# A four-layer graph network on one core: edges counted and ranked on TensorE, given rows filled in between the first scatters, blank rows given different indices

## The chip, the cores and the metric

The kernel runs on one core of one Trainium2 chip. The metric is the device time of one execution in microseconds (us); it is read beside one profiled execution, whose trace gives start, duration and releaser of every instruction.

## The reference

There are 3,125 nodes with 160 features (64 scalars and 32 vectors of 3) and 100,000 edges with a source and a destination; the destinations are sorted, the sources random. Four graph layers follow each other, each on the normalized and rectified node features, and each adds to the node features. What matters here is the common pattern:

```python
h = jnp.maximum(_layernorm(x, axis=-1), 0.0)
w = act(edge_features @ W_fc1) @ W_fc2           # layers 0, 1, 3
y = (h @ W)[gather_index]                        # a row of the node table per edge
m = products(w, y, edge_vector)                  # message of each edge
agg = segment_sum(m, scatter_index, num_segments=N)
x = x + combine(agg @ W_out, h @ W_skip)
```

Layer 0 sums over the source and gathers by the destination; layers 1 to 3 gather by the source and sum over the destination.

## The kernel before, in words

Nodes are split into bins of 32 (`BINS` is 100). Edges must lie in *tiles* of 128 that touch one bin only, so that a one-hot matrix of 128 x 32 on TensorE can sum them. There are 880 tiles in 110 groups of 8. A tile that is not full ends in *blank rows*, with key -1; tiles that no bin needs are blank in whole and stand last. Edges are held as 128 partitions by 782 columns, cut into 34 *chunks* of 23 columns (`CHUNK`, `CHUNKS`).

**Prologue.** VectorE finds for every edge its slot (`pos_i`). `places(o)` counts the edges of every bin per partition (L1011, one compare with an accumulated sum for each of 100 bins), TensorE sums the counts over partitions (L1402, L1403), and VectorE works out the first slot of every bin and the tables of tiles. `rank` then goes over the bins in fours: a mark of 0 or 1 (L1058), a running sum of the marks that starts at the bin's base (L1062, into PSUM), the last column carried to the next segment (L1069), and a copy of the sums where the mark is set (L1070). The 782 columns are ranked in three *segments*, which end at chunks 6, 18 and 34 (`SEGMENTS`); `positions` turns ranks into slots. Order o = 0 is by source, o = 1 by destination.

With the slots, ScalarE's `fill` puts edge vector, index and key into a staged chunk (L794 to L800), and GpSimd's `scatter` writes it, one indirect DMA of 128 rows per column (L670, 782 in all), into `rows_a`, which a large DMA on ScalarE's queue has cleared to blank rows (L751, semaphore `s_init`). SP stages the chunks (`stage_rows`, L530). The rows of layers 1 to 3 are already sorted: `given` on SP (L481 load, L485 store) and `complete` on ScalarE (L761, L763) put index and key into each chunk of them and store it to `rows_given`, two buffers in turn; `copy_tiles` later copies runs of 128 of these into tiles (L463). Tiles without edges copy a blank row block. `starts` and `bins_out` on SP send the tables of tiles through DRAM (L506, L520, L521, L523). ScalarE goes on to the chunks from the seventh (`COPY_FROM`) only after segment 1, all given rows and the tile starts (`s_starts`). If the destinations are not sorted (`flag`), the second order is ranked too, and placed by GpSimd. From chunk 18 on, node statistics and the first node table are worked out beside the fills.

**Layers.** In each, an edge phase of 110 groups: SP loads a group of rows, GpSimd gathers 8 times 128 rows of the node table by their index (L739), ScalarE turns marks into selections (L866), TensorE makes weights and sums (L1484, L1507, L1509, in layer 2 L1503), VectorE the products (L1209, L1213) and the sum over tiles (L1197). Two buffers of 8 tiles hold the gathered rows. A node phase follows (L1549, L1557). Queues work in program order; all waits are semaphores written by hand.

The few lines that set the order around the change, on DVE:

```python
places(0)
segment(0)
# falls, then
places(1)
segment(1)
segment(2)
statistics()
prep_first()
```

Of the kernel before, what the change touches and what calls it, by code (L numbers as in the profile page):

```python
# [55 lines left out]
WAYS = 4  # L56
assert BINS % WAYS == 0
WORK = 2 * PRODS * 320 + 2 * 1024
assert WORK >= 2 * PRODS * 416 + 2 * 512
PREP_FROM = SEGMENTS[2]  # L60

# [146 lines left out]
def gnn_program(nc, t):  # L208

    ctx = ExitStack()  # L210
    with ctx:
# [71 lines left out]
        def bank(i, p, a, b):  # L283
            return pb[i][0:p, a:b]
# [17 lines left out]
        eq = [carve(even // 2).bitcast(I16)[:, 0:COLS] for _ in range(WAYS)]  # L302
        zero_h = carve(even // 2).bitcast(I16)[:, 0:COLS]
# [4 lines left out]
        pos_f = [sh2[:, k * COLS:k * COLS + COLS] for k in range(3)] + [carve(COLS)]  # L308
        tri, ones = carve(P), carve(P)
        count, ntile, first_tile, bins_f, bins_z, pad = (carve(BINS) for _ in range(6))  # L310
        base = [carve(BINS) for _ in range(2)]
# [5 lines left out]
        bins_i = carve(BINS).bitcast(I32)  # L317
        tile_id, tile_bin = carve(TCOLS), carve(TCOLS)
        tile_bin_i = carve(TCOLS).bitcast(I32)
# [5 lines left out]
        s_in = sem("s_in")  # L325
# [15 lines left out]
        s_cnt = [sem(f"s_cnt{o}") for o in range(2)]  # L341
        s_cum = [sem(f"s_cum{o}") for o in range(2)]
        s_eq = [sem(f"s_eq{o}") for o in range(2)]
        s_scan = [sem(f"s_scan{o}") for o in range(2)]
        s_pick = [sem(f"s_pick{o}") for o in range(2)]
# [6 lines left out]
        s_again = sem("s_again")  # L352
# [11 lines left out]
        s_ranked = sem("s_ranked")  # L364
# [105 lines left out]
        def _(sp):  # L470
            sp.dma_start(key_i[0], t["skey"]).then_inc(s_in, 16)
            sp.dma_start(sh, t["edge_attr_3"]).then_inc(s_in, 16)
            sp.dma_start(key_i[1], t["dkey"][0:P * COLS].rearrange("(p c) -> p c", p=P)).then_inc(s_in, 16)
            sp.dma_start(key_next, t["dkey"][1:P * COLS + 1].rearrange("(p c) -> p c", p=P)).then_inc(s_in, 16)
# [27 lines left out]
            def bins_out(o):  # L502

                sp.wait_ge(s_tb[o], 1)
                with nc.allow_non_contiguous_dma(reason="one word per tile"):
                    sp.dma_start(bins_dram[o].rearrange("(c p) -> p c", p=P), tile_bin_i).then_inc(s_tbd[o], 16)  # L506
# [18 lines left out]

# [1113 lines left out]
```

## Time and profile before

| | |
|---|---|
| median of 3 runs | 6326.96 us (6325.39 to 6328.03) |
| profiled execution | 6318.5 us |
| its span | 6316.5 us |
| busy TensorE / VectorE | 4116.9 / 3529.7 us |
| busy ScalarE / GpSimd | 3434.8 / 4217.4 us |
| mean DMA traffic | 80 GB/s |
| first scatter / first gather | 251.4 / 1359.6 us |

The busy times are sums over stages with different limits. The span is to be read in stages: the prologue up to the last scatter, then four times an edge phase and a node phase. PE is TensorE, DVE is VectorE, ACT ScalarE, POOL GpSimd, SP the engine that only issues DMAs; a q behind a name is its queue. Durations of GpSimd's instructions are those of issuing the DMA, not of its transfer.

### The profile page before, as it was taken

How to read it: one execution, taken by the hardware profiler on the slowest of the kernel's cores; microseconds unless marked ns; L12 is line 12 of the kernel's file. 1: busy time of each engine (PE TensorE's matmuls, PEld its weight loads, DVE VectorE, ACT ScalarE, POOL GpSimd, SP SyncE). 2: the span in 40 equal slices, each digit the busy share in tenths (PEclk: the TensorE clock that was granted, in tenths of full speed). 3: DMA queues.
4: the chain of work that ended last, by engine and by line, in shares of the span. 5: the costliest groups of instructions: out<-in, count | busy, mean ns of one | idle time of the engine just before them, and what ended most of it. 6: DMA issues, size and time to landing. Idle time of an engine off the chain costs nothing.

```text
span 6316.5 us, 109949 instructions
## 1 busy us (share of the span) xinstructions
PE 4116.9 (65%) x22628; PEld 3645.2 (58%) x22628; DVE 3529.7 (56%) x10802; ACT 3434.8 (54%) x14704; POOL 4217.4 (67%) x4426
## 2 busy tenths in 40 slices
PE   0000011129999998799999986454545588888887
PEld 0000001129988887688888875444444577777776
DVE  8899400038877776466666655233233356666666
ACT  0000000016666664488888876666666467777773
POOL 2355777767777775177777764777777457777772
PEclk9999999999999999899999997555555699999998
DMA  8321223324444446022222252222222422222234
GB/s 314 109 44 45 71 75 80 77 61 94 94 91 93 92 92 70 27 79 78 79 78 78 79 68 56 79 79 78 79 79 79 43 64 79 78 78 79 79 76 38
DMA packets 660093, 506.69 MB, mean 80 GB/s; under 512 B 445302, under 2 KB 563333, under 8 KB 659894
## 3 DMA queue, kind: packets, MB, share of 16 engines
q0 software_dynamic: 195888, 316.94, 21.5%
q1 hardware_dynamic: 381782, 148.41, 9.7%
q10 hardware_dynamic: 82352, 40.52, 2.2%
q8 instruction: 29, 0.48, 0.0%
q14 instruction: 42, 0.34, 0.0%
HBM read 423.69 MB, written 96.48 MB: 82 GB/s over the span
## 4 chain that ended last, share of the span: by engine, by line
POOL 29%; issue 19%; DMA 13%; PE 11%; DVE 4%; DVEq 1%; SPq 1%; ACT 1%; POOLq 1%; ACTq 0%
POOL gath L739 29%; DMA gath<-table,rows 9%; PE bank L1557 2%; DMA rows<-rows_b 2%; PE bank L1507 2%; PE bank L1484 2%; PE bank L1549 1%; DVE work L1213 1%; DMA rows<-rows_a 1%; PE bank L1509 1%; PE bank L1503 1%; DVE acc L1197 1%; DVE work L1209 1%; DVEq L1220 0%; PE bank L1457 0%
## 5 line engine op out<-in xcount | busy, mean ns | idle before, releaser
L739 POOL DMA_INDIRECT gath<-table,rows x3520 | 3356.7, 954 | 1223.3 <-issue 1004.0
L866 ACT ACTIVATE sel<-acc,rows 128x32 f32<-128x32 f32 x10560 | 2294.1, 307 | 713.0 <-DVE acc L1188 712.2
L1197 DVE TENSOR_TENSOR acc<-acc,bank 128x160 f32 (+1 forms) x3520 | 1208.3, 343 | 1068.7 <-PE bank L1503 704.4
L1507 PE MATMUL bank<-work,sel 128*128 128x160 f32 (+1 forms) x5280 | 1341.5, 336 | 95.9 <-DVE acc L1197 94.7
L1484 PE MATMUL bank<-w,work 128*128 128x224 f32 (+2 forms) x5280 | 1169.0, 344 | 114.3 <-DVE work L1213 104.2
L1509 PE MATMUL bank<-work,sel 128*128 128x160 f32 x5280 | 1156.6, 301 | 0.0
L670 POOL DMA_INDIRECT rows_a<-acc x782 | 770.2, 985 | 528.7 <-ACT acc L800 291.0
L1484 PEld LDWEIGHTS bank<-w,work 128*128 128x128 f32 (+1 forms) x5280 | 894.5, 192 | 261.5 <-DVE work L1213 192.5
L1507 PEld LDWEIGHTS bank<-work,sel 128*128 128x128 f32 x5280 | 886.7, 191 | 193.4 <-DVE acc L1197 167.7
L1209 DVE TENSOR_TENSOR work<-bank,gath 128x256 f32<-128x256 f32 x1320 | 555.7, 421 | 775.2 <-DMA gath<-table,rows 715.6
L1509 PEld LDWEIGHTS bank<-work,sel 128*128 128x128 f32 x5280 | 915.9, 192 | 46.3
L1503 PE MATMUL bank<-gath,sel 128*128 128x160 f32 x1760 | 549.0, 493 | 575.1 <-DMA gath<-table,rows 559.7
L1213 DVE TENSOR_TENSOR work<-bank,gath 128x192 f32<-128x192 f32 (+1 forms) x2640 | 895.3, 381 | 0.0
L1503 PEld LDWEIGHTS bank<-gath,sel 128*128 128x128 f32 x1760 | 462.1, 330 | 661.9 <-issue 645.0
L866 ACT ACTIVATE sel<-sel,rows 128x32 f32<-128x32 f32 x2640 | 581.7, 308 | 53.3 <-DVE sel L1188 45.3
L1377 PE MATMUL bank<-ident,sel 128*64 128x128 f32 x25 | 10.2, 407 | 791.4 <-ACT sel L777 791.4
L1377 PEld LDWEIGHTS bank<-ident,sel 128*64 128x64 f32 x25 | 4.3, 173 | 794.2 <-issue 794.1
L849 ACT ACTIVATE work<-bank 100x512 f32<-100x512 f32 (+1 forms) x440 | 250.9, 596 | 352.3 <-PE bank L1457 229.9
L794 ACT ACTIVATE acc<-acc 128x69 f32 (+1 forms) x34 | 9.3, 273 | 773.6 <-DMA acc<-in_rows_a 583.9
L844 ACT ACTIVATE attrT<-bank 128x256 f32<-128x256 f32 (+1 forms) x330 | 145.4, 441 | 270.4 <-PE bank L1447 226.8
L1460 PE MATMUL bank<-attrT,w 128*100 128x256 f32 x880 | 210.9, 383 | 1.8 <-ACT attrT L844 1.8
L1011 DVE TENSOR_SCALAR_CACHE_REDUCE acc<-acc,iota_bins 128x782 int16<-128x782 bf16 x200 | 193.6, 1024 | 26.5 <-DVE acc L1011 25.8
(216 smaller groups left out, 2961.0 us busy)
## 6 DMA issues: line engine op xcount, KB each, us to landing
gath<-table,rows POOLq DMA_INDIRECT x3520
rows<-rows_b SPq DMA_DIRECT2D x330, 128.0 KB
rows_a<-acc ACTq DMA_DIRECT2D x1, 30360.0 KB, 111.5
rows<-rows_a SPq DMA_DIRECT2D x110, 256.0 KB
acc<-in_rows_a SPq DMA_DIRECT2D x34, 793.5 KB, 4.5
acc<-in_rows_b SPq DMA_DIRECT2D x34, 368.0 KB, 3.5
rows_given<-acc SPq DMA_DIRECT2D x34, 368.0 KB, 3.9
rows_a<-acc POOLq DMA_INDIRECT x782
```

The lines of the kernel that those rows point to most:

```text
L670: pool.indirect_dma_start(rows_dram[0][:, :], bass.IndirectOffsetOnAxis(ap=pos_r[q][:, u:u + 1], axis=0), stage[0][q][:, u * A_W:(u + 1) * ...
L739: pool.indirect_dma_start(gath[q][:, u, :], None, table_dram[n][:, :], bass.IndirectOffsetOnAxis(ap=flat[:, u * w + first:u * w + first + ...
L849: i = act.activation(hid_t(n, q)[0:hrows, 512 * b:512 * b + 512], bank(2 + b, hrows, 0, 512), ACT.Silu if n == 3 else ACT.Relu, scale={0: ...
L866: i = act.activation(sel[q][:, t, at:at + BIN], hot, ACT.Copy, scale=e[:, k:k + 1])
L1197: dve.tensor_tensor(sums, sums, bank(6 + b, P, 256 * h, 256 * h + L.width), ALU.add).then_inc(S["fl"].sem, 1)
L1209: dve.tensor_tensor(ps, wt[:, :, 0:128].rearrange("p h (w c) -> p h w c", w=2), two[:, :, 0:S0].unsqueeze(2).to_broadcast([P, 2, 2, S0]), ...
L1213: ins = dve.tensor_tensor(pv, wt[:, h, 128:L.wcols].rearrange("p (w m) -> p w m", w=nv) .unsqueeze(2).to_broadcast([P, nv, 3, V1]), two[:, ...
L1460: i = pe.matmul(bank(2 + k // 2, 100, 256 * (k % 2), 256 * (k % 2) + 256), w1[1][:, k, :], attrT[:, 0:256], start=True, stop=True)
L1484: ins = pe.matmul(bank(4 + u % 2, P, 224 * h, 224 * h + L.wcols), hid, w, start=True, stop=True, skip_group_check=True)
L1503: ins = pe.matmul(out, sel[qv][:, t, 0:128], gath[qv][:, t, :], start=True, stop=True, skip_group_check=True)
L1507: pe.matmul(out, sel[qv][:, t, 96:224], work[:, a + NF:a + NF + L.width], start=True, stop=False, skip_group_check=True)
L1509: ins = pe.matmul(bank(6 + b, P, 256 * h, 256 * h + NF), sel[qv][:, t, 0:128], work[:, a:a + NF], start=False, stop=True, skip_group_check ...
```

## The change

**Counting.** A mark (`mark`, L1034 of the kernel after) is one compare into one of 8 bfloat16 buffers in `work`. For each bin TensorE multiplies the 782 marked columns by a matrix whose only column of ones is the bin's (`one_at`, L1438, L1439), so that two PSUM banks collect a count per bin and column over all partitions. VectorE runs the sum along the columns (`bases`, L1066, L1068), gets the tiles per bin, has TensorE sum those, and subtracts the columns' own counts, which gives a base per bin and column.

**Ranking.** For each bin TensorE multiplies the marks by a triangle of ones in bfloat16 (`tri_h`, L1459), which counts the marked edges in the partitions above, and adds the bin's row of bases in float32 (L1460); VectorE copies the result where the mark is set (L1122), now into one array `pos_f`. Four PSUM banks and a lead of four marks stand between them. The scans, the carries, the four partial arrays and their clearing go. The segments end at chunks 4, 18 and 34.

**Order.** VectorE waits for the source keys alone before it counts; the work on the edge vectors lies between the marks of the first count. The second order is always ranked, before the node statistics. SP loads the first chunks and the nodes first, and starts the given rows after `s_init`; ScalarE completes 10 given chunks after its second fill and 6 after each of the third to sixth.

**Blank rows** get an index of their own, 3(8p + t) for partition p and tile t of a group, in place of 0.

```diff
-SEGMENTS = (0, 6, 18, CHUNKS)
-COPY_FROM = SEGMENTS[1]
+SEGMENTS = (0, 4, 18, CHUNKS)
+COPY_FROM = 6
+GIVEN_FIRST, GIVEN_EACH = 10, 6
+MARKS, PREFIXES, AHEAD = 8, 4, 4
+PAD_STEP = NODES // (P * GT)
...
+            for o, k in enumerate((A_IDX, B_IDX)):
+
+                pool.iota(blank[o].rearrange("p (t c) -> p t c", t=GT)[:, :, k].bitcast(I32), pattern=[[PAD_STEP, GT]], base=0,
+                          channel_multiplier=PAD_STEP * GT).then_inc(s_blank, 1)
...
-            sp.wait_ge(s_in, 64)
-            pipeline(sp, CHUNKS, 2, 0, 1, given)
+            for c in range(2):
+                stage_rows(c, 0, c)
...
+            sp.wait_ge(s_init, 16)
+            step = 0
+            for c in range(2, COPY_FROM):
+                for _ in range(GIVEN_FIRST + 1 if c == 2 else GIVEN_EACH):
+                    given(step, step // 2, step % 2)
+                    step += 1
+                stage_rows(c, c // 2, c % 2)
+            for step in range(step, CHUNKS + 1):
+                given(step, step // 2, step % 2)
...
+            def mark(o, b, lo, hi):
+
+                e = marked[0]
+                wait(dve, s_used, e - MARKS + 1)
+                dve.tensor_scalar(marks[e % MARKS][:, 0:hi - lo], bin_h[o][:, lo:hi], iota_bins[:, b:b + 1], None,
+                                  ALU.is_equal).then_inc(s_mark, 1)
+                marked[0] += 1
...
+            def rank(o, lo, hi):
+
+                first = marked[0]
+                for b in range(BINS + AHEAD):
+                    if b < BINS:
+                        mark(o, b, lo, hi)
+                    if b >= AHEAD:
+                        r = picked[0]
+                        mask = marks[(first + b - AHEAD) % MARKS].bitcast(I16)[:, 0:hi - lo]
+                        wait(dve, s_prefix, r + 1)
+
+                        wait(dve, s_pick, r)
+                        dve.copy_predicated(pos_f[:, lo:hi], mask, bank(4 + r % PREFIXES, P, 0, hi - lo)).then_inc(s_pick, 1)
+                        picked[0] += 1
+                wait(dve, s_pick, picked[0])
...
+            count(0)
+            bases(0)
...
             segment(0)
-
+            tiles(0)
+            segment(1)
...
+            count(1)
+            bases(1)
+            tiles(1)
             segment(2)
+            for half in range(2):
+                rank(1, half * (COLS // 2), (half + 1) * (COLS // 2))
+            positions(1, 0, COLS)
+            dve.wait_ge(s_pos[1], 1)
...
+            def rank(o, lo, hi):
+
+                for b in range(BINS):
+                    wait(pe, s_mark, used[0] + 1)
+                    wait(pe, s_pick, ranked[0] - PREFIXES + 1)
+                    out = bank(4 + ranked[0] % PREFIXES, P, 0, hi - lo)
+                    pe.matmul(out, tri_h, marks[used[0] % MARKS][:, 0:hi - lo], start=True, stop=False).then_inc(s_used, 1)
+                    pe.matmul(out, ident[0:BINS, b:b + 1].to_broadcast([BINS, P]), base[o][0:BINS, lo:hi],
+                              start=False, stop=True).then_inc(s_prefix, 1)
```

SP's queue at the start of the program, before (the given rows are loaded into and stored from `acc`; between these rows the loop over the other given chunks is left out):

```order
L474 DMA acc<-in_dkey 128x782
L481 DMA acc<-in_rows_b 128x736 x2
L485 DMA rows_given<-acc 128x736
...
L489 DMA x<-in_x 128x25x160
L492 DMA attr<-in_node_vec 128x25x1
L506 DMA tile_bins<-acc 128x7x1
L530 DMA acc<-in_rows_a 128x1587 x2
```

The same place in the kernel after, up to the third chunk's load and then from the last given stores to the tables:

```order
L486 DMA acc<-in_dkey 128x782
L492 DMA acc<-in_rows_a 128x1587 x2
L507 DMA x<-in_x 128x25x160
L510 DMA attr<-in_node_vec 128x25x1
L499 DMA acc<-in_rows_b 128x736 x2
L503 DMA rows_given<-acc 128x736
...
L492 DMA acc<-in_rows_a 128x1587
...
L503 DMA rows_given<-acc 128x736 x2
L534 DMA tile_bins<-acc 128x7x1 x2
L548 DMA tile_starts<-acc 128x7x1
```

The rows of the first two chunks and the nodes moved ahead of the given rows, and the tables of tiles to behind all of them.

VectorE in the ranking of the first segment, before, the end of one round over four bins (the scans write `bank`, a PSUM bank each):

```order
L1058 TENSOR_SCALAR acc<-acc,iota_bins 128x138
L1062 ISA
L1062 SCALAR_TENSOR_TENSOR bank<-acc 128x138
...
L1069 COPY acc<-bank 128x1
L1070 COPY_PREDICATED acc<-acc,bank 128x138
```

And after, from the bases (L1066 to L1080) into the ranking (`work` holds the marks):

```order
L1066 SCALAR_TENSOR_TENSOR work<-bank,acc 100x512
L1068 SCALAR_TENSOR_TENSOR work<-bank,work,acc 100x270
...
L1076 TENSOR_SCALAR acc<-bank 100x1
L1080 SCALAR_TENSOR_TENSOR acc<-work,acc,bank 100x92
...
L1034 TENSOR_SCALAR work<-acc,iota_bins 128x92 x5
L1122 COPY_PREDICATED acc<-work,bank 128x92
```

Of four instructions per bin two are left, and what they read from `bank` now comes from TensorE's L1459 and L1460.

## Rows read from the trace of the kernel before

**Rows 1.** Page, costliest groups: GpSimd's gathers; busy us, mean ns, idle before.
```profile
L739 POOL DMA_INDIRECT gath<-table,rows x3520 | 3356.7, 954 | 1223.3 <-issue 1004.0
```

**Rows 2.** Timeline of GpSimd, 250:555: start us, us, line, [idle before <-releaser].
```profile
251.40 1.29 POOL L670 DMA_INDIRECT rows_a<-acc  x1 [196.97 <-ACT acc L800]
...
522.48 1.15 POOL L670 DMA_INDIRECT rows_a<-acc  x1 [94.03 <-ACT acc L800]
```

**Rows 3.** Windows, the scatters alone: stretch, us, busy, clock, DMA share, GB/s.
```profile
554.00:709.00 155.00, 120.14 (x115) 1.00 0.28 70
710.00:1350.00 640.00, 486.69 (x504) 1.00 0.30 75
```

**Rows 4.** Timeline of VectorE, 11:250.
```profile
11.13 2.60 DVE L963 TENSOR_TENSOR acc<-acc 128x2346 f32<-128x2346 f32 x1 [11.00 <-DMA acc<-in_dkey]
...
25.19 0.71 DVE L1090 MEMSET acc<- 128x782 f32 x1 [0.23 <-DVE acc L967]
...
142.74 0.26 DVE L1016 TENSOR_SCALAR acc<-bank 128x100 int32<-128x100 f32 x1 [1.33 <-PE bank L1403]
...
249.17 0.30 DVE L1086 TENSOR_TENSOR acc<-acc 128x138 int32<-128x138 int32 x1
```

**Rows 5.** Groups by shape, VectorE, 0:700: marks L1058 and picks L1070.
```profile
L1070 DVE COPY_PREDICATED acc<-acc,bank 128x368 f32<-128x368 int16 x100 | 47.4, 550 | 0.0
...
L1070 DVE COPY_PREDICATED acc<-acc,bank 128x138 f32<-128x138 int16 x100 | 28.1, 302 | 0.0
...
L1058 DVE TENSOR_SCALAR acc<-acc,iota_bins 128x368 int16<-128x368 bf16 x100 | 25.6, 319 | 10.5 <-DVE acc L1070 10.2 <-DVE acc L1086 0.2
...
L1058 DVE TENSOR_SCALAR acc<-acc,iota_bins 128x138 int16<-128x138 bf16 x100 | 19.1, 256 | 12.8 <-DVE acc L1070 12.5 <-issue 0.2
```

**Rows 6.** Timeline of TensorE, 2060:2066, edge phase 0 at full clock.
```profile
2061.18 0.59 PE L1507 MATMUL bank<-work,sel 128*128 128x256 f32 x2
2061.61 0.43 PE L1509 MATMUL bank<-work,sel 128*128 128x160 f32 x2
```

**Rows 7.** Page, DMA issues: KB each, median us from issue to landing.
```profile
rows_a<-acc ACTq DMA_DIRECT2D x1, 30360.0 KB, 111.5
...
acc<-in_skey SPq DMA_DIRECT2D x1, 391.0 KB, 3.1
```

**Rows 8.** Timeline of SP's queue, 20:410: given-row loads, tile tables, next rows.
```profile
27.23 0.36 SPq L481 DMA_DIRECT2D acc<-in_rows_b  x1
...
109.87 0.34 SPq L481 DMA_DIRECT2D acc<-in_rows_b  x1
...
213.39 0.34 SPq L481 DMA_DIRECT2D acc<-in_rows_b  x1
...
370.67 0.38 SPq L506 DMA_DIRECT2D tile_bins<-acc  x1
383.37 0.38 SPq L520 DMA_DIRECT2D tile_starts<-acc  x1
...
400.46 0.38 SPq L530 DMA_DIRECT2D acc<-in_rows_a  x1
```

**Rows 9.** Windows, GpSimd, in edge phase 1: middle and end.
```profile
3600.00:3650.00 50.00, 37.82 (x41) 1.00 0.28 78
3720.00:3785.00 65.00, 38.32 (x41) 0.89 0.90 56
```

**Rows 10.** Timeline of GpSimd, 6143:6218, the last 47 gathers of phase 3.
```profile
6143.81 0.95 POOL L739 DMA_INDIRECT gath<-table,rows  x1 [0.30 <-issue]
...
6217.22 0.95 POOL L739 DMA_INDIRECT gath<-table,rows  x1 [0.30 <-issue]
```

**Rows 11.** Chain that ended last, 6120:6225: start us, us, what.
```profile
6132.54 2.54 DMA gath<-table,rows
...
6212.18 9.65 DMA gath<-table,rows
```

**Rows 12.** Windows, all engines, edge phase 2; clock behind the busy times.
```profile
3900.00:4900.00 1000.00, 497.91 (x1599) 419.20 (x1598) 300.21 (x995) 686.28 (x3191) 757.20 (x797) 0.50 0.28 78
```

More of the change, by code:

```diff
@@ L572, in _ @@
             bins_out(0)
-            for c in range(2):
-                stage_rows(c, 0, c)
-            pairs(sp, 2, COPY_FROM, stage_rows)
             bins_out(1)
@@ L1028, in places, with tiles @@
+            def tiles(o):
+                dve.wait_ge(s_rows, o + 1)
+                link(dve.tensor_copy(ntile, bank(3, P, 0, BINS)))
+                link(dve.tensor_copy(first_tile, bank(3, P, 128, 128 + BINS)))
                 for c in range(TCOLS):
@@ L1392, in prep_first @@
                 pipeline(pe, BLOCKS, 3, 2, 1, body)
-            for o in range(2):
-                if o:
-                    pe.wait_ge(s_falls, 1)
-                    pe.matmul(bank(1, 1, 0, 1), falls, ones[:, 0:1], start=True, stop=True).then_inc(s_flag_sum, 1)
-                    pe.wait_ge(s_tb[0], 1)
-                pe.wait_ge(s_cnt[o], BINS)
-                pe.matmul(bank(0, P, 0, BINS), tri, count, start=True, stop=True)
-                pe.matmul(bank(0, P, 128, 128 + BINS), ones, count, start=True, stop=True).then_inc(s_cum[o], 1)
+            used, ranked = [0], [0]
@@ new lines, in count @@
+            def count(o):
+                for b in range(BINS):
+                    wait(pe, s_mark, used[0] + 1)
+                    seen = marks[used[0] % MARKS]
+                    row = one_at[:, BINS - 1 - b:2 * BINS - 1 - b]
+                    pe.matmul(bank(0, BINS, 0, BANK), row, seen[:, 0:BANK], start=b == 0, stop=b == BINS - 1)
+                    ins = pe.matmul(bank(1, BINS, 0, COLS - BANK), row, seen[:, BANK:COLS], start=b == 0, stop=b == BINS - 1)
+                    ins.then_inc(s_used, 1)
+                    used[0] += 1
+                pe.wait_ge(s_total, o + 1)
+                pe.matmul(bank(2, BINS, 0, 1), tri[0:BINS, 0:BINS], tiles_of[0:BINS, :], start=True, stop=True).then_inc(s_first, 1)
@@ new lines, in rank @@
+            def rank(o, lo, hi):
+                for b in range(BINS):
+                    wait(pe, s_mark, used[0] + 1)
+                    wait(pe, s_pick, ranked[0] - PREFIXES + 1)
[3 more added lines that the diff above has]
+                              start=False, stop=True).then_inc(s_prefix, 1)
+                    used[0] += 1
+                    ranked[0] += 1
@@ new lines, in _ @@
+            count(0)
+            pe.wait_ge(s_base[0], 1)
+            rank(0, 0, SEGMENTS[1] * CHUNK)
+            rows_of(0)
+            pe.wait_ge(s_base[0], 3)
+            rank(0, SEGMENTS[1] * CHUNK, SEGMENTS[2] * CHUNK)
+            pe.wait_ge(s_falls, 1)
+            pe.matmul(bank(3, 1, 0, 1), falls, ones[:, 0:1], start=True, stop=True).then_inc(s_flag_sum, 1)
+            count(1)
+            rows_of(1)
+            rank(0, SEGMENTS[2] * CHUNK, COLS)
+            pe.wait_ge(s_base[1], 3)
@@ L1405, in _ @@
+            for half in range(2):
+                rank(1, half * (COLS // 2), (half + 1) * (COLS // 2))
             pe.wait_ge(s_flag, 1)
```

235 lines of the change are left out of this document (113 added, 122 removed).

## Prediction

> **What bounds the kernel now.** I first asked which engine has no slack. In the costliest groups GpSimd's gathers stand alone: 3,520 of them at 954 ns, and most of the idle time before them is called issue, 1004.0 us [rows 1], 0.30 before each [rows 10]. So one gather costs 1.255 us, 47 of them 59, and the four edge phases (880 each) run at GpSimd's pace. Ahead of them stand the 782 scatters. GpSimd's timeline shows the first at 251.40 after 196.97 us of idling, and another stop of 94.03 before 522.48, between the 138th and the 139th; ScalarE ended both [rows 2]. Undisturbed, a scatter takes 640/504 = 1.27 us, a chunk of 23 of them 29.2; while VectorE ranks the last segment it is 155/115 = 1.35 [rows 3]. 251.4 + 94 + 34 x 29.2 + 11 for the disturbed chunks is 1349 (by the same sum 1149 after), and edge phase 0 follows. So the prologue is worth two stops, and what sets them is VectorE, which counts and ranks until 249.17 [rows 4] and again before the second stop. The last place is the end of each edge phase, below.
>
> **Counting and ranking, up to the first scatter.** Sizes 138 and 368 give prices [rows 5]. A mark (compare, bfloat16 in, 16 bits out) takes 191 to 256 ns of VectorE, 0.28 ns a column: 178 ns for 92 columns, 243 for 322, 262 for 391, 373 for 782. 
>
> VectorE no longer waits for all four loads (11.00 us [rows 4]): the source keys land 3.1 us after an issue at 0.9 [rows 7], and two casts make it 6. Marks: 100 x 0.373 = 37. The edge-vector work, 11.13 to 25.19 [rows 4], is only moved in between: 14. Bases: eight short instructions at the 0.26 us of L1016, one round trip through TensorE at its 1.33 us [rows 4], and 1,564 columns of scan and subtraction, which I put at 2 ns each: 6.5. Ranking four chunks, not six: 100 x (0.178 + 0.252) = 43. Positions, six instructions of 0.25: 1.5. From their end to the first scatter it was 249.47 to 251.40, 1.9. Sum: 6 + 37 + 14 + 6.5 + 43 + 1.5 + 1.9 = 110. The clearing of the scattered rows took until 2.4 + 111.5 = 114 [rows 7], beside ten given-row steps that now wait for it; so it ends earlier, and is the second limit. I take 111. **Gain: 251.4 - 111 = 140.** Bounds: 98 (no gap between instructions, half the bases) and 131 (slow TensorE).
>
> **The second stop.** Segment 1 (14 chunks) needs 100 x 0.74 = 74 and is ranked by about 190; the chunks before it last until 111 + 4 x 29.2 = 228. That stop goes. What is late next is SP's queue. The given-row steps, once ahead of the ranking, now lie after the first two fills, behind the wait for the clearing, and SP cannot send the tile tables before the last of them. A step took (213.39 - 109.87)/22 = 4.7 us without the clearing beside it, and (109.87 - 27.23)/9 = 9.2 with it [rows 8]. From the second fill at 112: 34 x 4.7 = 160, so 272; chunks 2 to 5 come in time, since each needs six steps, 28 us, of a 29.2 us chunk. Then the first tile table, 12.7, and from the second table's issue to the next load of rows 400.46 - 370.67 = 29.8 [rows 8]; in both kernels ScalarE's seventh fill needs all that. With the load (under one step, 4.7) and the fill, 1.9: 321. GpSimd is through six chunks at 111 + 175 = 286. **Stop 35 for 94: gain 59.** Bounds: 0 and 80. VectorE's part of the tables (second count, bases, tiles: 55 us after segment 1) is done by 245, 40 before SP asks for it; were SP faster, the stop would end with VectorE, near 0.
>
> The second ranking, once skipped for sorted keys, now always runs: 2 x 100 x 0.84 = 168 us. VectorE is then free at about 495; the node preparation needs it at chunk 18, 321 + 12 x 29.2 = 671. Hidden by 176 us. Nothing on GpSimd's own queue changes but two short iotas and the blank index columns. The disturbed scatters: 115 x 0.08 = 9 us before; after the stop 170 us of ranking remain at the same 6%: 10. **Zero.** The Trainium skill, SBUF — State Buffer, section "Who interferes with whom", says that a VectorE compare in a 2-port mode shuts GpSimd out for the whole instruction, and descriptor writing with it. By it the stretch would be dearer than the rows say; that is a rival.
>
> **Blank rows.** They all held source index 0, now 128 different ones. About 40 wholly blank tiles end each edge phase. There the DMA engines are busy 0.90 of the time for 56 GB/s, against 0.28 for 78 in the middle of the phase, and GpSimd issues 41 gathers in 65 us, not in 50 [rows 9]: the transfers are slow, not many. In the last phase the 47 gathers from 6143.81 to 6217.22 take 73.4 us instead of 59, 14.4 too many [rows 10]; the same two rows of the other three give 19.5, 14.5 and 14.9. Sum 63. A late gather then lands 9.65 us after its start, an ordinary one 2.54 [rows 11]; some 5 of these 7 us are left at each end, 20. I take all of it, as the index is the one thing that sets these rows apart. **Gain: 83.** Bounds: 0 and 92.
>
> **Sum.** 6318.5 - 140 - 59 - 0 - 83 = 6036.5 by the profiled execution's own time. The median of the runs stands 8.5 above it, so 6045. No change could be told from one of 0.2%, about 13 us.
>
> **Rivals.**
> - *TensorE stays at the low clock in the prologue.* In edge phase 2 it is busy 498 of 1000 us and granted 0.50, 1.2 GHz [rows 12]; in ranking 92 columns it would be busy under half of the time. Against it: counting keeps it busy 0.33 of 0.37 us, and while it idles in the scatters the page still prints 1.00 [rows 3], which settles nothing. At half the clock counting takes 65 us, 322 columns 134: first scatter at 131, segment 1 at 275 against 248, tile tables only at 352, seventh chunk at 387 instead of 321: +66, 6111. Chance 0.10. The Trainium skill, TensorE: Matmul & The Clock Gate, Part 1, says that the low clock is the default and work releases it; the trace agrees as far as phase 2 goes.
> - *Given-row steps slowed by the scatters beside them*, at 6 to 9.2 us instead of 4.7: 34 times 1.3 to 4.5, +45 to +150, 6090 to 6195. For it the 9.2 beside the clearing; against it, the scatters load the engines far less. Chance 0.10.
> - *GpSimd shut out by every mark.* 200 marks of 0.26 us in the stretch after the stop are 52 instead of 10: +42, 6087. The scatters at 1.35 us [rows 3], beside as many marks as that per column, speak against it. Chance 0.06.
> - *Blank rows were not the cause*, the slow tails stay: 6045 + 83 = 6128. Chance 0.06.
> - *The stop vanishes too* (the small tables land faster once nothing is queued ahead): 6010. Chance 0.05.
> - *Slower than before: the hand-over doesn't pipeline.* VectorE and TensorE now exchange two signals per bin in 700 bins; four banks and a lead of four marks hide this. If every pick waited for a round trip, 1.33 us [rows 4] beside its own work, VectorE would be free only at 25 + 700 t, and the 15 chunks from the node preparation on come after it, 440 us. That passes the old end of 1353 plus the 83 of the tails from t = 1.4 us a bin; at 1.7 it ends at 1655, +505 against my 1150: 6550. The lead in the code speaks against it. Chance 0.03.
>
> **Chances.** The forecast itself has 0.60, within 6005 to 6080 by its own bounds. The range that leaves out 2 in 10 takes in the vanished stop, the shut-out and part of the slow steps and the low clock: 5995 to 6112. Faster 0.96, same 0.01, slower 0.03.
>
> **What would show it.** First scatter near 111 (98 to 131); 0.37 us per mark of 782 columns and TensorE not ending VectorE's waits in counting; one stop near 35 us before the 139th scatter, ended by ScalarE with the tile tables behind it; the last scatter near 1150; the 47 last gathers of each phase in 59 to 62 us, at a DMA share near 0.3. A first scatter past 131, steps over 5 us on SP, or tails still at 73 us would make it wrong.

## The result, and the profile after

The changed kernel takes **6037.2 us** (median of 4 runs, 6032.0 to 6039.1) against 6326.2 us before (6323.1 to 6328.0): ratio **0.954, interval 0.9525 to 0.9553**. The forecast was 6045, range 5995 to 6112. The profiled execution has a span of 6037.4 us, 279.1 less than before.

Two of the four terms came out as forecast, one was 16 us too large, and one of zero was a net gain of 9. Timeline of GpSimd after the change (start us, us, line, operation, idle before and its releaser), at the first scatter, at the stop between the 138th and the 139th, at the last scatter and at the last gather:

```profile
127.53 1.10 POOL L697 DMA_INDIRECT rows_a<-acc  x1 [67.81 <-ACT acc L824]
...
342.38 0.97 POOL L697 DMA_INDIRECT rows_a<-acc  x1 [35.27 <-ACT acc L824]
...
1160.76 0.97 POOL L697 DMA_INDIRECT rows_a<-acc  x1 [0.30 <-issue]
1168.28 1.00 POOL L766 DMA_INDIRECT gath<-table,rows  x1 [6.55 <-DMA rows<-rows_a]
...
5945.32 0.95 POOL L766 DMA_INDIRECT gath<-table,rows  x1 [0.30 <-issue]
```

The first scatter moved from 251.40 to 127.53 (-123.9), the wait of 94.03 became 35.27 [rows 2], the last scatter moved from 1352.4 to 1160.76 (-191.6), the last gather from 6217.22 [rows 10] to 5945.32. The wait is ended by the same partner as before, ScalarE's fill. Of the 191.6 the first scatter gives 123.9 and the stop 58.8. The other 9 are a difference: the scatters behind the stop, which the ranking no longer disturbs, take 11.5 us less, and the first 138 take 2.5 us more than before (experiment 3 says why). From the last scatter to the last gather it took 4864.8 us and now takes 4784.6 (-80.2), and from there to the end 99.3 and now 92.1 (-7.2).

Windows of GpSimd (stretch, its length, busy with count, granted clock, DMA share, GB/s), first two with scatters, where rows 3 stood at 115 and 504 of them, then the middle and the end of edge phase 1, where rows 9 stood at 0.28 and 0.90:

```profile
554.00:709.00 155.00, 117.81 (x123) 0.50 0.30 73
710.00:1130.00 420.00, 319.35 (x331) 0.50 0.32 78
...
3000.00:3050.00 50.00, 37.84 (x40) 1.00 0.31 77
3490.62:3548.62 58.00, 43.98 (x46) 1.00 0.29 77
```

The last 47 gathers of the four phases take 59.1, 59.2, 59.1 and 59.3 us, before 79.1, 73.5, 73.9 and 73.4; the DMA engines are now no busier there than in the middle.

SP's queue before the stop (start us, us, line, what moves):

```profile
294.59 0.33 SPq L499 DMA_DIRECT2D acc<-in_rows_b  x1
295.03 4.19 SPq L503 DMA_DIRECT2D rows_given<-acc  x2
299.27 12.92 SPq L534 DMA_DIRECT2D tile_bins<-acc  x2
321.05 0.36 SPq L548 DMA_DIRECT2D tile_starts<-acc  x1
321.46 2.85 SPq L549 DMA_DIRECT2D tile_first_node<-acc  x1
334.75 0.29 SPq L551 DMA_DIRECT2D acc<-tile_starts  x1
336.51 0.41 SPq L492 DMA_DIRECT2D acc<-in_rows_a  x1
```

The last given rows are stored at 295 to 299 (forecast 272, from a start at 112); then three landings of small tables follow each other, and only then come the rows of the seventh chunk. The forecast's order is there, 20 us later, as its start is 16 later.

**Why the first scatter is at 127.5 and not at 111.** Timeline of VectorE, ahead of the count, between count and ranking, and at the end of the first segment:

```profile
4.31 5.31 DVE L1056 TENSOR_SCALAR acc<-acc 128x782 int32<-128x782 int32 x1 [4.18 <-POOL acc L662]
...
10.26 3.10 DVE L1034 TENSOR_SCALAR work<-acc,iota_bins 128x782 bf16<-128x782 bf16 x9
...
60.57 1.22 DVE L1066 TENSOR_TENSOR_SCAN work<-bank,acc 100x512 f32<-100x512 f32 x1 [0.63 <-PE bank L1439]
...
65.33 0.86 DVE L1034 TENSOR_SCALAR work<-acc,iota_bins 128x92 bf16<-128x92 bf16 x5
...
123.92 0.26 DVE L1122 COPY_PREDICATED acc<-work,bank 128x92 f32<-128x92 int16 x1 [0.32 <-PE bank L1460]
```

The count starts at 10.26 and not at 6: a shift of 782 integers takes 5.31 us beside GpSimd's fillings (4.22 to 9.79 us), where the like of it at 49.19 takes 0.56. Count and edge vectors take 50 us against 51, the bases 4.8 against 6.5. Then a hundred bins of 92 columns take 58.9 us against 43, and the picks wait for TensorE. Windows of all engines (TensorE's matmuls and weight loads, VectorE, ScalarE, GpSimd, then clock): the whole count, a part of it, the gap behind it, the first ranking, and the second segment's:

```profile
10.00:60.00 50.00, 39.91 (x198) 21.65 (x199) 49.06 (x107) 0.85 (x1) 44.04 (x74) 0.93 1.07 388
36.00:42.00 6.00, 5.63 (x17) 3.57 (x18) 5.55 (x16) 0.00 (x0) 6.00 (x10) 0.50 1.08 391
64.00:65.00 1.00, 0.00 (x0) 0.00 (x0) 0.96 (x4) 0.00 (x0) 0.00 (x0) 0.50 1.07 389
66.00:73.00 7.00, 7.00 (x37) 6.98 (x38) 4.81 (x25) 0.00 (x0) 0.00 (x0) 0.50 1.06 383
73.00:106.00 33.00, 33.00 (x172) 32.89 (x172) 23.27 (x115) 0.00 (x0) 0.00 (x0) 0.50 0.93 331
136.00:138.00 2.00, 2.00 (x11) 1.22 (x10) 2.00 (x7) 0.04 (x1) 1.39 (x3) 1.00 0.87 314
```

In the ranking TensorE is busy without a gap and granted 0.50, the 1.2 GHz level: 0.59 us a bin. The clock had fallen before the ranking's first product at 65.72, in the gap. The count has a smaller case of the same: VectorE's reciprocal (30.82 to 35.86 us) leaves TensorE with 1.5 us of work between 30 and 36, and 36 to 42 is granted 0.50. Groups by shape in 66:123 (busy us, mean ns, idle before and releasers):

```profile
L1460 PE MATMUL bank<-acc,ident 100*128 100x92 f32 x198 | 57.5, 458 | 0.0
...
L1122 DVE COPY_PREDICATED acc<-work,bank 128x92 f32<-128x92 int16 x98 | 25.5, 260 | 17.2 <-PE bank L1460 17.1
L1034 DVE TENSOR_SCALAR work<-acc,iota_bins 128x92 bf16<-128x92 bf16 x97 | 23.4, 242 | 0.0
```

VectorE waits 17.2 us for the bases' float32 matmul. Against the forecast's terms that is +4.3 (start), -0.7 (count), -1.7 (bases), +15.9 (bins), -0.1 (positions and fill): 17.6 over their sum of 109.9, 16.5 over the 111 taken.

### The profile page after: what moved, and what is told of

Same layout as the page of the kernel before. It is cut to its first block, busy times and chain, and to the rows that moved or that the text cites. A ratio compares the mean times of both kernels' runs of the same rounds, so it can differ in the third digit from the quotient of the medians.

```text
span 6037.4 us, 112434 instructions
## 1 busy us (share of the span) xinstructions
PE 4551.9 (75%) x24536; PEld 3911.6 (65%) x24536; DVE 3374.1 (56%) x10505; ACT 3437.0 (57%) x14704; POOL 4216.1 (70%) x4431
## 4 chain that ended last, share of the span: by engine, by line
POOL 26%; issue 17%; PE 15%; DMA 13%; DVE 5%; DVEq 2%; ACT 1%; SPq 1%; POOLq 1%; ACTq 0%
POOL gath L766 26%; DMA gath<-table,rows 11%; PE bank L1582 3%; PE bank L1559 3%; DMA rows<-rows_a 2%; PE bank L1632 2%; PE bank L1584 2%; DVE work L1249 2%; PE bank L1578 2%; PE bank L1624 1%; DVE acc L1233 1%; PE bank L1535 1%; DVEq L1256 1%; DVE work L1245 1%; ACT sel L900 0%
## 5 line engine op out<-in xcount | busy, mean ns | idle before, releaser
L1460 PE MATMUL bank<-acc,ident 100*128 100x391 f32 (+3 forms) x1000 | 374.5, 475 | 0.0
L1122 DVE COPY_PREDICATED acc<-work,bank 128x391 f32<-128x391 int16 (+3 forms) x500 | 253.1, 506 | 34.0 <-PE bank L1460 29.6
```

What stands on the lines that cost most here:

```text
L1122: dve.copy_predicated(pos_f[:, lo:hi], mask, bank(4 + r % PREFIXES, P, 0, hi - lo)).then_inc(s_pick, 1)
L1460: pe.matmul(out, ident[0:BINS, b:b + 1].to_broadcast([BINS, P]), base[o][0:BINS, lo:hi], start=False, stop=True).then_inc(s_prefix, 1)
```

## The experiments

Where nothing else is said, the kernel before took 6320 to 6326 us beside the runs.

### 1. TensorE kept at work between count and ranking

The last product of the count ends at 60.5 us and the first of the ranking starts at 65.7; between them TensorE had 0.5 us of work. Fourteen products into a spare bank fill the gap:

```diff
                     ins.then_inc(s_used, 1)
                     used[0] += 1
+                if o == 0:
+                    for _ in range(8):
+                        pe.matmul(bank(3, P, 0, BANK), tri_h, bin_h[0][:, 0:BANK], start=True, stop=True)
                 pe.wait_ge(s_total, o + 1)
                 pe.matmul(bank(2, BINS, 0, 1), tri[0:BINS, 0:BINS], ...).then_inc(s_first, 1)
+                if o == 0:
+                    for _ in range(6):
+                        pe.matmul(bank(3, P, 0, BANK), tri_h, bin_h[0][:, 0:BANK], start=True, stop=True)
```

> The changed kernel with 14 more bf16 products of 512 columns on TensorE, 8 between the last count and the tiles' sum and 6 behind it, into a spare bank, in the 5 us in which TensorE has almost nothing to do before the first ranking. Theory (the granted clock fell to 0.50 at 73.2 us because TensorE had a gap from 60 to 65 us, and the low clock is why a bin of the first ranking takes 0.58 us instead of 0.43): clock at 1.00 to the end of the first segment, first scatter at 111 to 114 us instead of 127.5; then the first chunks are 15 us earlier, but the stop in front of chunk 6, which ends by SP's queue, takes all of it back: 6037 within 5 us. Rival 1 (the clock falls because of the short float32 products, gap or no gap): first scatter at 127 to 131 us. Rival 2 (the end follows the first scatter, not the queue): 6022.

Measured: 6013.9 us (6012.9 to 6015.2), ratio 0.9514 (0.950 to 0.9529), 23 us under the change as made. The two intervals just overlap (the change as made starts at 0.9525), so what carries this experiment is its trace. Windows of this kernel at the start of the ranking and over it (it ends at 102.4), then the groups:

```profile
66.00:73.00 7.00, 7.00 (x64) 6.60 (x62) 7.00 (x40) 0.00 (x0) 0.00 (x0) 1.00 1.06 380
66.00:102.00 36.00, 35.71 (x301) 32.70 (x299) 35.30 (x194) 0.00 (x0) 0.00 (x0) 1.00 1.04 374
```

```profile
L1466 PE MATMUL bank<-acc,ident 100*128 100x92 f32 x200 | 35.9, 293 | 0.0
...
L1122 DVE COPY_PREDICATED acc<-work,bank 128x92 f32<-128x92 int16 x99 | 25.7, 260 | 0.7 <-PE bank L1466 0.3
```

The granted clock stays at 1.00 (2.4 GHz) through the ranking, although its products are the same short ones; the matmul takes 293 ns and not 458, VectorE's wait is gone, and the hundred bins take from 64.87 to 102.4 us, 0.375 each instead of 0.59. First scatter at 106.12: 21 us earlier, more than expected, as mark and pick follow each other faster than their two durations (0.242 + 0.260) add up to. The profiles repeat it: in the three kernels with the fourteen products the first scatter is at 106.1 to 106.3, in all those that rank and count as changed without them, and keep the order of the given rows, at 127.0 to 127.5. So the gap lowered the clock, and the short float32 products alone don't. The first half of the theory holds. (The expectation says 73.2 us for the fall; the windows show it between 62 and 64 us.) The Trainium skill, TensorE: Matmul & The Clock Gate, Part 1, has the half rate as the state that idleness brings back; by that rule and these windows alike, the work goes into the gap, and not into the ranking. The section also lets activity release the throttle, and there the trace is less simple: the ranking kept TensorE busy all through 66 to 123 us at 0.50, and the clock was back only at 136, beside the next segment's products.

Its second half fell: I expected the stop to take the 21 us back. Its length nearly stayed (61.7 us from the sixth chunk's start to the seventh's, 64.6 in the change as made), and the scatters came 21 us earlier at the first and 24 at the last. The given steps don't start with the clearing but with ScalarE's `complete`, which stands behind the second fill and so behind the ranking; an earlier first scatter moves the whole queue, tables and all.

### 2. The stop before the seventh chunk

First, the small tables between the given steps instead of behind them (SP's order alone, landings waited for where the data are read):

```diff
                 stage_rows(c, c // 2, c % 2)
+                if c == 3:
+                    bins_out(0)
+            bins_out(1)
+            starts_out()
             for step in range(step, CHUNKS + 1):
                 given(step, step // 2, step % 2)
+            starts_in()
```

> The changed kernel with the tile tables' writes issued between the given steps (the bins of ranking 0 after chunk 3's rows, the bins of ranking 1 and the starts after chunk 5's rows, at about 270 us), their landings waited for only where the data are read. Theory (the second stop of 35 us is the queue of SP: six given steps of 5 us from 270 to 295 us and behind them three table landings to 335 us, one behind the other): tables land beside the last steps, the starts row at about 302 to 306 us, chunk 6's first scatter at about 308 to 314 us instead of 342, and 6037 - 28 to 35 = 6002 to 6009 us. Rival (the tables are slow because the DMA engines are full, and only get slower between the given steps): the steps stretch, the scatter of chunk 6 stays at 335 to 342 us, 6030 to 6040 us. Second rival (the scatters are not what the end follows): scatter earlier, time at 6037.

Measured: 6027.5 us (6024.9 to 6031.3), ratio 0.9536 (0.9523 to 0.9549), within the interval of the change as made. In the profile the seventh chunk starts at 328.1 instead of 342.4, but the fourth, fifth and sixth chunk take 33.2, 38.3 and 39.7 us. SP's queue there:

```profile
273.50 0.87 SPq L510 DMA_DIRECT2D tile_bins<-acc  x1
274.41 0.89 SPq L516 DMA_DIRECT2D tile_starts<-acc  x1
275.35 0.88 SPq L517 DMA_DIRECT2D tile_first_node<-acc  x1
276.90 2.56 SPq L499 DMA_DIRECT2D acc<-in_rows_b  x1
287.91 0.35 SPq L503 DMA_DIRECT2D rows_given<-acc  x1
299.96 0.33 SPq L499 DMA_DIRECT2D acc<-in_rows_b  x1
```

The load behind the tables is issued at 276.90 and the next at 299.96, where two steps take 10 us: the tables, one word to each address, cost the given steps 13 us. Of the 28 to 34 us that the theory gave the seventh chunk 14 are left, and in the time they are within the noise.

Then the same four writes on ScalarE's queue, together with experiment 1:

```diff
+                    if c == COPY_FROM - 1:
+                        act.wait_ge(s_start, 1)
+                        act.dma_start(starts_dram.rearrange("(c p) -> p c", p=P), tile_start).then_inc(s_startd, 16)
+                        act.dma_start(first_node_dram.rearrange("(c p) -> p c", p=P), tile_node).then_inc(s_startd, 16)
```

> The changed kernel with the 14 products that fill TensorE's gap, and with the four writes of tile tables (bins, starts, first nodes) issued on ACT's queue behind the rows of chunks 4 and 5 instead of on SP's behind the last given steps. Theory (the gap costs 21 us at the first scatter and all scatters after it, and the stop in front of chunk 6 comes from four one-word-per-tile writes that stand in SP's queue, 10 to 13 us each, after the last given step): first scatter at 106 us, the given steps end at 274 us as without the tables' move, the starts row is read at about 277 us, chunk 6's first scatter at 287 to 292 us instead of 318.6, so 6014 - 26 to 31 = 5983 to 5988 us. Rival (the small writes hold the DMA engines, whichever queue they stand in, as they did between the given steps, where three in a row took 23 us out of the given steps): chunk 6 at 305 to 312 us, 6002 to 6010 us.

Measured: 6019.8 us (6013.4 to 6023.4), ratio 0.9511 (0.9498 to 0.9524); experiment 1 alone had 0.9514. The rival's mechanism holds, and it costs more than the rival said (6002 to 6010 us). SP's queue, with the tables now on the other one (one issued at 222.46, the other three from 262.17 on):

```profile
259.23 0.33 SPq L499 DMA_DIRECT2D acc<-in_rows_b  x1
265.04 0.34 SPq L503 DMA_DIRECT2D rows_given<-acc  x1
284.83 0.33 SPq L499 DMA_DIRECT2D acc<-in_rows_b  x1
```

25.6 us between two loads that are otherwise 5 apart: the writes are no dearer for standing in SP's queue, they hold up the given steps from the other queue too. The seventh chunk starts at 315.1, 3.5 us before that of experiment 1, and not at 305 to 312. The Trainium skill, DMA: Bandwidth & Descriptors, Specifications, gives 512 bytes as the least size of a transfer at full rate, since shorter ones are read, modified and written; these have 4. No run here separates that cause from another, but it fits a cost that goes where the writes go.

Last, the seventh chunk ahead of the tables, again with experiment 1. Its scatter reads nothing of them, only the copies of whole tiles do:

```diff
+            stage_rows(COPY_FROM, COPY_FROM // 2, 0)
             bins_out(0)
             bins_out(1)
             starts()
...
             assert done == CHUNKS
+            fill(COPY_FROM, COPY_FROM // 2, 0)
             act.wait_ge(s_empty, 16)
```

> The changed kernel with the 14 products that fill TensorE's gap (alone 6014 us), and with the rows and the fill of chunk 6 put ahead of the tile tables in SP's and ACT's order; only the copies of whole tiles still wait for the tables and the given rows. Theory (chunk 6 waits for the tables by the order of the two queues alone, since its scatter reads nothing of them, and the small writes cost the same 36 us wherever they stand, but now beside chunk 6's scatter): chunk 6 starts at 286 to 289 us instead of 318.6, chunk 7 follows at about 320 to 325 us (its rows stand behind the tables, which end at about 313 us), so 22 to 28 us of the 32 are kept: 6014 - 22 to 28 = 5986 to 5992 us. Rival (the small writes stretch chunk 6's rows and scatters as they stretched the given steps): chunk 7 at 335 us or later, 6000 to 6014 us.

Measured: 6016.7 us (5999.2 to 6019.5) where the kernel before took 6345.8, so a ratio of **0.9479 (0.9467 to 0.9492)**, the lowest of all: clearly under the change as made (0.9525 at least), and by little under experiment 1 (0.950 at least). Beside a kernel before of 6326 us that ratio is 5997 us, against an expected 5986 to 5992. The profiled execution, the lowest of the five, has a span of 5997.5 us. The seventh chunk starts at 285.2, with no stop; the stop is now before the eighth:

```profile
336.07 0.97 POOL L700 DMA_INDIRECT rows_a<-acc  x1 [21.69 <-ACT acc L827]
```

That is 11 us won and not 22 to 28. The small writes are little of the reason: from the first table's issue to the load of the starts they took 37.8 us, 35.5 in the change as made. SP's queue shows the rest:

```profile
313.85 0.29 SPq L551 DMA_DIRECT2D acc<-tile_starts  x1
317.39 12.47 SPq L475 DMA_DIRECT2D rows_b<-rows_given  x16
329.98 0.52 SPq L492 DMA_DIRECT2D acc<-in_rows_a  x1
```

Sixteen tile copies of the seventh chunk take 12.5 us to issue and stand ahead of the eighth chunk's rows. I had left these out of the expectation. Rows before copies would be the next step; that was not tried.

### 3. The old order around the given rows, and no second ranking

```diff
+            pipeline(sp, CHUNKS, 2, 0, 1, given)
...
-            for c in range(2, COPY_FROM):
-                for _ in range(GIVEN_FIRST + 1 if c == 2 else GIVEN_EACH):
-                    given(step, step // 2, step % 2)
...
+            pairs(act, 0, CHUNKS, complete)
             act.wait_ge(s_pos[0], 1)
```

> The changed kernel with the old order around the given rows: all 34 given steps before the first scatter, not waiting for the clearing, the rows of chunks 2 to 5 after them. The ranking stays as changed. Theory (the interleaving is worth what the given steps would take in front of the first scatter, less the second stop that it causes): the steps run from about 15 us at 4.7 us and more each, beside the clearing, to 190 to 215 us, the first scatter is at 195 to 220 us instead of 127, the stop in front of chunk 6 vanishes (35 us), so +33 to +58: 6070 to 6095 us. Rival (given steps are quick without scatters beside them and end by 130 us): the first scatter stays near 130 us and the stop goes, 6002 to 6015 us, faster than the change as made.

Measured: 6104.6 us (6102.7 to 6108.0), ratio 0.966. First scatter at 226.9, no stop at the seventh chunk, last scatter at 1224.3, 63.6 later than in the change as made: +99.4 at the front, -36 up to the 139th scatter. The direction is the theory's; the front is 7 us past its range, and the time 10, since the steps beside the clearing take 8.2 to 9.6 us each. The interleaving is worth 67 us, over a third of what the prologue gained; faster ranking alone would have left the given rows as the new first wait.

```diff
-            for half in range(2):
-                rank(1, half * (COLS // 2), (half + 1) * (COLS // 2))
             positions(1, 0, COLS)
```

> The changed kernel without the second ranking's 200 picks, marks and products (positions by destination, which are read only when the keys are unsorted; this run leaves them out). Theory (168 us of VectorE work lie wholly beside the scatters, which end at 1161 us): VectorE is done at about 345 us instead of 515, scatters keep 29.3-29.4 us each, and the time is 6037 within 6 us. Rival (the marks in bf16 shut GpSimd out of the shared port and stretch its descriptors): chunks during 345 to 515 us become shorter by 1 to 2 us each, 5 chunks, 6027 to 6032 us.

Measured: 6034.6 us (6032.0 to 6035.8), ratio 0.9547 (0.9532 to 0.9561): no change. Scatters beside the ranking and without it, first the change as made, then this kernel:

```profile
345.00:515.00 170.00, 129.44 (x134) 0.99 0.33 78
```

```profile
345.00:515.00 170.00, 129.35 (x134) 0.50 0.32 77
```

134 scatters in 170 us, 1.27 us each, both times. Some 200 marks of 0.33 us cost GpSimd nothing. Before the change the stretch beside VectorE's ranking had 1.35 us a scatter [rows 3]. Its timeline shows where: in every round of four bins one scatter's issue of five takes 1.39 us and not 0.97, and it is always the one that is under way as the four scans end. One round of the kernel before:

```profile
602.91 0.97 POOL L670 DMA_INDIRECT rows_a<-acc  x1 [0.30 <-issue]
603.35 3.61 DVE L1062 TENSOR_TENSOR_SCAN bank<-acc 128x368 f32<-128x368 int16 x4
605.46 1.39 POOL L670 DMA_INDIRECT rows_a<-acc  x1 [0.30 <-issue]
```

The long issue ends at 606.85, the scans at 606.96; the one at 602.91 runs beside marks (602.40 to 603.43) and takes the usual 0.97. All 20 rounds from 554 to 690 us look like this. So what is gone is the scans, and why they hold up an issue no run here shows.

Marks are not free everywhere. In the second count of the kernel after they follow each other without a gap, 782 columns wide, and there the scatters take 1.03 us to issue and 1.34 from one to the next:

```profile
213.05 28.87 DVE L1034 TENSOR_SCALAR work<-acc,iota_bins 128x782 bf16<-128x782 bf16 x86 [0.16 <-PE bank L1439]
216.29 1.03 POOL L697 DMA_INDIRECT rows_a<-acc  x1 [0.30 <-issue]
```

From 243 us on, with the count over and the DMA engines as busy, it is 1.27 again. That makes 1.8 of the 2.5 us that the first 138 scatters lost.

### 4. The blank rows

```diff
-            for o, k in enumerate((A_IDX, B_IDX)):
-                pool.iota(blank[o]..., pattern=[[PAD_STEP, GT]], base=0, channel_multiplier=PAD_STEP * GT).then_inc(s_blank, 1)
```

> The changed kernel with the blank rows naming node row 0 again, as before the change. Theory (the 5 per cent came from two places, and the blank rows are worth 83 to 92 us of it): the last 47 gathers of each edge phase go back from 59.1-59.3 us to 73.4-79.1 us, the transfers behind each phase grow by 5 to 7 us, and the run takes 6037 + 83 to 92 = 6120 to 6130 us; the first scatter stays at 127 us. Rival (the tails became shorter because the phases start and end at other moments, not by the blank rows): within 5 us of 6037.

> The kernel before the change with the spread blank rows alone. Theory (both gains add up, since the tails lie behind each other in the chain and nothing of the ranking reaches them): 6326 - 83 to 92 = 6234 to 6243 us, first scatter still at 251 us. Rival (the gain of the blank rows needs the new ranking): within 5 us of 6326.

> The changed kernel with all blank rows naming one node row in the middle of the table (5000) and not row 0. Theory (what costs is that all blank rows read the same row, whichever): tails of 73 to 79 us and 6120 to 6130 us, as with row 0. Rival (row 0 is special, by its place at the start of the table): 6037 us.

> The changed kernel with eight rows for the blanks: the 128 partitions of one gather all read the same row, the eight gathers of a group read eight rows that lie 1,250 apart. Theory A (it is the repeat inside one gather that costs, 128 descriptors on one row): as slow as with one row for all, tails of 73 to 79 us, 6120 to 6130 us. Theory B (it is the repeat over all transfers in flight, so one row in eight gathers is an eighth of the crowd): most of the gain stays, tails of 59 to 63 us, 6037 to 6055 us.

The middle row is 1562 and the eight rows lie 390 apart, since there are 3,125 nodes; the expectations name wrong numbers. These four were made in one session in which everything that moves data was slower: the kernel before took 8461.8 us (8426 to 8478), groups of gathers 12.9 to 15.1 us on average over a phase, instead of 10. They took 8381.5, 8428.5, 8357.3 and 8347.8 us. The second, the kernel before with spread rows, is faster by 33 us there (ratio 0.9972, 0.9955 to 0.999), not by 83 to 92, for at that pace 47 ordinary gathers take 76 to 89 us themselves, as long as the tails. What can still be read is edge phase 0: its last 47 gathers take 92.8 us with row 0, 90.7 with one row in the middle, 81.0 with eight rows and 79.1 spread (this last in the kernel before; the second and third come from one run each). By that, row 0 is not special. Whether the two gains add up as exactly as the theory says stays open at the ordinary pace; it wasn't tried again.

> The changed kernel with the blank rows naming node row 0 again, a second time: the first time the four runs on blank rows were made where the kernel before took 8462 us and a group of gathers 14.6 to 15 us, so that nothing of 6037 us can be read from them. Theory, as before: the last 47 gathers of each edge phase go back from 59.1-59.3 us to 73.4-79.1 us, and where the kernel before takes 6320 to 6326 us the run takes 6037 + 83 to 92 = 6115 to 6130 us. Rival (the tails are shorter by the phases' other timing): within 5 us of the change as made.

Measured: 6114.5 us (6106.7 to 6127.3), ratio 0.9671 (0.9655 to 0.9688), 77 us over the change as made. Tails of 86.3, 72.3, 77.6 and 74.0 us: +73.5 in sum, and the stretches behind the four phases are 5.7, 6.1, 1.9 and 5.5 us longer: 92.7. Against it stand a stop 7 us shorter and groups of gathers at 10.018 us instead of 10.061, 4 us a phase (last section). The profiled spans differ by 70.0.

> The changed kernel with eight rows for the blanks (one row for all 128 partitions of one gather, the eight gathers of a group on eight rows), a second time, where groups of gathers take 10 us. With row 0 for all the last 47 gathers take 86.3, 72.3, 77.6 and 74.0 us and the run 6114 us. Theory A (the repeat inside one gather costs, and row 0 is nothing special): tails of 72 to 86 us, 6105 to 6125 us. Theory B (the repeat over all transfers in flight costs, or row 0's place does): tails of 59 to 63 us, 6037 to 6055 us.

Measured: 6126.1 us (6122.9 to 6129.1), ratio 0.9653 (0.9638 to 0.9667), with the kernel before at 6345.8. The total fits A, the phases say something else. Tails of 60.5, 74.6, 75.3 and 75.8 us. Windows of GpSimd over the last 47 gathers of phases 0 and 1:

```profile
2239.52:2298.72 59.20, 44.47 (x47) 1.00 0.64 88
3501.60:3574.93 73.33, 43.94 (x47) 0.86 0.82 56
```

and phase 0 with row 0 everywhere:

```profile
2225.82:2310.86 85.04, 43.83 (x47) 0.86 0.79 60
```

Only phase 0 reads the eight rows. In layers 1 to 3 blank tiles are copies of one 128-row block of `rows_given`, made from the first of the eight columns (`blank[1][:, 0:B_W]`), which in this variant is row 0 throughout. So phase 0 is the test, and it says B: 128 descriptors on one row cost 1.4 us over the spread rows in 47 gathers, if the next gather goes to another row; the DMA engines are still twice as busy (0.64 for 88 GB/s). Phases 1 to 3 repeat the case of row 0. In the change as made these phases read 128 rows, the same in all eight gathers (24p by the change's formula, not 3(8p + t)), and are fast.

## Why the prediction was right, point by point

- **First scatter, gain 140: it was 123.9.** The step "Then TensorE needs 0.33 us per bin in counting ..." held in counting (the marks wait 0.7 us for TensorE there), and the choice of the lower price was right for wide products at the high clock. The term that was mis-sized is "Ranking four chunks, not six", 100 x (0.178 + 0.252) = 43 by VectorE alone: it was 58.9, by TensorE at 0.50. Two things make that up. First, "width is what it pays for" fails for narrow products: by width 92 columns would cost TensorE 0.20 us a bin and 0.39 at the low clock, both under VectorE's 0.43, so that the forecast's prices show no harm here at either clock; measured are 0.30 (experiment 1, first bins) and 0.58. At 322 columns and the low clock width still holds (1.34 us a bin). The weight loads are as busy as the products in the narrow ranking (32.89 of 33 us); whether they set the 0.58 is not shown. Second, the low clock, which I had as a rival for the whole prologue at 0.10, came for a part of it: from the gap behind the count into the first bins of segment 1, and the windows from 136 to 200 us stand at 1.00 again, so segment 1 was ranked in time. The rival's reason (too little to do in ranking) is not the cause: experiment 1 has as little to do and keeps the clock. The other part of the miss is the start of the count, 4.3 us.
- **Second stop, gain 59: it was 58.8**, for the reasons given: ScalarE's fill, behind SP's tables, behind the given rows. Both ends of the stop, forecast at 286 and 321, came 21 us later, 16.5 of it by the late ranking. That the remaining 4 to 5 us are equal is luck: in front it is slower scatters, at the back 34 given steps that took 172 us and not 160 (5.0 each, against 4.7) and tables and fill that took 43 and not 49.
- **Second ranking, zero: right** (experiment 3). **Disturbed scatters, zero: they gave 9 us.** I carried the 6% over to the new kernel, taking VectorE's work as one thing; it had been the scans. The rival of the marks that shut GpSimd out, 0.26 us each, did not come: the Trainium skill, SBUF — State Buffer, "Who interferes with whom", would have a compare in a 2-port mode block GpSimd's descriptor writing; the scatters keep 1.27 us beside 200 marks of 391 columns. They don't beside gapless marks of 782, but even there, with a mark every 0.34 us, an issue is longer by 0.06 only. Which mode the marks ran in is not shown.
- **Blank rows, gain 83: 63.2 in the tails and 25.9 at the four ends, 89.1**, against 63 and 20 (the 19.5 of phase 0 is 20.1 by its rows). Putting them back costs 92.7 in the same places, and 70 to 77 of the time.
- The sum, 6036.5, is for the profiled execution's own time, which was 6039.1. That it is off by 2.6 only is luck in part: 16 us missing at the first scatter stand against 9 of the scatters and 4 behind the last one. The median, forecast 8.5 above the sum, lies 2 under that execution, so 6045 is 8 too high.

## What to carry to other kernels

A short idle stretch of TensorE can cost more behind it than in it: when its work is a chain of short products right after a gap, look at the granted clock there, and fill the gap rather than the chain. And price a narrow product by a narrow one in a trace, not by its width. When several transfers feed padding, give the padding different addresses, and check every place from which padding is copied. And before moving a slow little transfer elsewhere, ask whether it is its place that costs or the transfer; here only work put ahead of it helped, and only as far as nothing else stood between.

## What the runs showed that I had not expected

- Adding the two iotas makes every gather's issue on GpSimd some 7 ns longer, whatever the blank indices are: the median is 948 ns before and 946 and 947 with the iotas out of the changed kernel, 953 to 957 in all kernels with them, the kernel before with spread rows (955) and the one-row variant (955) included. Against the changed kernel without them the groups are longer by 0.04 us of 10, 18 us over the kernel; against the kernel before it is half of that. What in the instruction stream does it is open.
- Four tables of 3.5 KB, written one word per address, take as long as seven given steps of 368 KB each way: 36 us from 299 to 335.
- The first integer shift of 782 columns takes 5.31 us on VectorE and ends as GpSimd's memory fillings end; a like instruction 45 us later takes 0.56. That the one holds up the other is argued from this, and wasn't tried.
- One session ran the kernel before in 8462 us instead of 6326, with GpSimd's own durations unchanged (951 ns a gather) and the transfers slower: chunks of scatters 41 us instead of 29. Only the kernel before beside each run tells such a session from an effect.
